# Graph attention by gathered rows, and a reordered first feed-forward stage, in a two-layer gated mixer on one Trainium2 core

## The chip, the core and the metric

The kernel runs on one core of one Trainium2 chip. The metric is the device time of one execution in microseconds (us). The core has five engines with an instruction stream each: TensorE (PE, matmuls into PSUM), VectorE (DVE), ScalarE (ACT, activations), GpSimd (POOL, which also issues indirect DMAs) and SyncE (SP, which issues the plain DMAs). The streams meet only in semaphores.

## The reference, cut to what matters

Inputs are x [4, 256, 256] and a context [4, 256, 64]; the tokens are 1024 rows, which the kernel holds as T = 8 tiles of 128. Four residual steps follow each other, each scaled with the tanh of a gate:

```python
x = x + tanh(g_xattn[0]) * graph_attention(ctx, layernorm(x))   # two layers, 8 heads of 32
x = x + tanh(g_ffn[0])   * ternary_ffn(layernorm(x))            # 256 -> 704 -> 256, silu(g) * u
x = x + tanh(g_xattn[1]) * learned_adjacency(ctx, layernorm(x))
x = x + tanh(g_ffn[1])   * moe(layernorm(x))                    # 8 experts, top 2, 256 -> 512 -> 256

# one graph layer; adj is layernorm(x), N x N
e = leaky_relu(attn_self[:, :, None] + attn_neigh[:, None, :]) + MASK_VAL * (1.0 - adj)
out = elu(softmax(e) @ feat + b)          # MASK_VAL = -1e10

# learned adjacency: sim is N x N per batch from two 64 x 64 products of the context
threshold = top_k(sim, 76)[..., -1:]
A = sigmoid(sim) * (sim >= threshold)
out = (1 - gamma) * adj + gamma * (A + A.T) / 2
```

With a mask of 1e10 times the entry, the softmax of the graph attention is 1 at the largest entry of the row of `adj` and 0 elsewhere as long as that entry leads by enough. So each graph layer gives node n the features of the one node idx(n), the position of the largest entry in row n. Both kernels use this, and check on the chip that it holds; if it does not, they branch to a general path, which this input never takes.

## The kernel before, in words

The first three steps run over all tokens in two halves of four tiles (HT = 4, HN = 512 tokens); a half is two of the four batches. The order of all of it is one list, SCHEDULE (L333), written out by hand: every engine walks the same list and issues its own part of each step that has one, so on every engine an instruction waits behind all that stands before it in the list. On VectorE, a second list, FILL (L767), puts steps of the top-k search behind named steps.

Graph part. `pick h` (VectorE) takes the LayerNorm of x, scales it to the mask, finds each row's maximum and writes `hot`, the one-hot matrix. `graph_hot` transposes it on TensorE. `graph_first` gathers the context rows by a matmul with it, `graph_hidden` is the first layer's product with its exp on ScalarE, `hidden_elu` its ELU, `graph_feat` (L1353, four tiles of 272 columns) the second layer's product, `graph_out` (L1363) gathers those rows, again by a matmul; `graph_elu` and `add_graph` end it. `logit_check` looks at the logits' size. `graph_check h` turns a flag into a branch on TensorE, ScalarE and VectorE, once per half: VectorE writes `flag` at L1045, then loads it and branches.

Learned adjacency, beside this. `queries` and `sims` compute `sim` for all tokens (ScalarE copies it out). The threshold is found by guess and correction: `spread` takes each row's mean and variance, `count n` (ScalarE, L584, one activation with a sum per tile) counts the entries above the guess, `move n` corrects it; then the search of `below` (five steps for each pair of tiles and a closing one, 21 in all) takes the top 16 below the guess. `lost` and `keep 0` check that the threshold is among them, with a branch around a full search that is written out for eight tiles (`search_in_full`, L850), and multiply the mask in. `sigmoids` (L589) is a tanh, a copy. `kept h` transposes the result.

Feed-forward part. `norm_ffn h` normalises, `turn_ffn h` transposes on TensorE and copies on ScalarE. `ffn_up h it` (TensorE L1448, ScalarE silu L655, VectorE gate L1066) is one of six up products of a half: four matmuls of 512 columns, two for the last. A product needs the gate of the product two before it, since it has two PSUM banks. The gate of the second half has one wait more:

```python
                if h == 1:
                    dve.wait_ge(down_done, 1)
```

since it overwrites `hT`, which the down product of the first half still reads. `ffn_down p` is the down product (L1467, 24 matmuls of 256 columns per half); VectorE multiplies it with `dsr` and adds it to x (L1084, L1088). Parts p are the first half, and two quarters of the second. `attn_stats`, `attn`, `moe_stats`, `norm_moe`, `turn_moe`, `router` and `choices` follow, the first half's beside the second half's up products.

POOL raises variances to the power -1/2 (L459) for each LayerNorm, and to 1/2 once for `spread` (L455), in a fixed order. SP loads all inputs, then experts 0 and 1; experts 2, 3, 4 and 7 wait for `graph_over` (both halves' graph part added), 5 and 6 for the last down product, as the FFN's weights lie in their place.

The expert part (L1150 onward in VectorE, L1520 onward in TensorE) sorts tokens into blocks, gathers each block's rows by indirect DMA and runs 19 blocks. The change does not touch it.

## Time and profile before

| what | us |
|---|---|
| median of 3 runs | 289.89 (289.8 to 295.19) |
| profiled execution | 290.8 |
| its span in the trace | 289.1 |
| TensorE busy | 231.3 |
| VectorE busy | 129.6 |
| ScalarE busy | 71.1 |
| POOL busy | 68.4 |
| first FFN up product starts | 62.60 |
| first down product | 87.92 to 98.55 |
| second down product | 124.57 to 135.21 |
| first gather of the expert part starts | 163.75 |

The span runs from the first to the last instruction of the profiled execution; its own time is 1.7 us longer than the span. "Busy" is the time in which an instruction of that engine runs; a busy matmul row is not TensorE at its peak, since a row's end is modelled.
### The profile page before, as it was taken

The numbers are of one execution on the slowest core, as the hardware profiler recorded it, in microseconds if no ns is written. First come the engines' busy times: TensorE is split into PE (matmuls) and PEld (weight loads), VectorE is DVE, ScalarE is ACT, GpSimd is POOL, SyncE is SP. The second block draws the span as 40 slices with busy tenths as digits, with TensorE's granted clock in tenths as the row PEclk, the third lists the DMA queues.
The fourth block names the chain that finished last, engine by engine and source line by source line (L and its number), as shares of the span: only waits on it lengthen the run. The fifth ranks groups of instructions, "written<-read, shape, count | busy, mean of one in ns | idle before, by whom it ended". The sixth has DMA issues, their size and how long they took to land.

```text
span 289.1 us, 3573 instructions
## 1 busy us (share of the span) xinstructions
PE 231.3 (80%) x1246; PEld 180.7 (63%) x1247; DVE 129.6 (45%) x407; ACT 71.1 (25%) x144; POOL 68.4 (24%) x84
## 2 busy tenths in 40 slices
PE   3979996469988997997071269999999999999950
PEld 3648575344347743575061169998999999986540
DVE  2779558779884478236948832000100100100100
ACT  1444654531120021200032011232123123123210
POOL 5010200100100011000210211355345435545442
PEclk9999999658999999999655559999999999999995
DMA  6797000009920002201950010223322422311200
GB/s 172 268 363 291 0 1 0 3 15 356 415 88 2 0 2 74 73 0 39 362 180 0 19 39 20 36 36 51 63 36 36 60 42 36 53 24 19 25 5 1
DMA packets 15829, 23.88 MB, mean 83 GB/s; under 512 B 4989, under 2 KB 11648, under 8 KB 15808
## 3 DMA queue, kind: packets, MB, share of 16 engines
q1 hardware_dynamic: 10400, 19.02, 18.2%
q0 software_dynamic: 3744, 4.20, 9.1%
q10 hardware_dynamic: 1664, 0.40, 0.6%
q8 instruction: 11, 0.18, 0.3%
q14 instruction: 10, 0.08, 0.1%
HBM read 20.07 MB, written 4.59 MB: 85 GB/s over the span
## 4 chain that ended last, share of the span: by engine, by line
PE 65%; DVE 19%; DMA 4%; issue 3%; POOL 3%; ACT 2%; DVEq 1%; POOLq 0%; ACTq 0%
PE PS L1551 19%; PE PS L1560 9%; PE PS L1467 7%; PE PS L1456 6%; PE PS L1566 4%; DMA zc<-xn_rows,idsu 3%; PE PS L1358 3%; DVE stat L753 2%; PE PS L1436 2%; PE PS L1291 2%; PE PS L1503 2%; PE PS L1544 2%; DVE xn L1055 2%; DVE hT L1074 2%; PE PS L1349 1%
## 5 line engine op out<-in xcount | busy, mean ns | idle before, releaser
L1551 PE MATMUL PS<-hT,e 128*128 128x128 f32 x512 | 64.0, 280 | 0.5 <-ACT hT L681 0.5
L1551 PEld LDWEIGHTS PS<-hT,e 128*128 128x128 f32 x512 | 62.3, 196 | 1.6 <-ACT hT L681 0.9
L1273 DVE TENSOR_TENSOR hT<-th,PS 128x512 f32<-128x512 f32 x19 | 13.1, 687 | 87.9 <-PE PS L1551 73.0
L1456 PE MATMUL PS<-xnT,e 128*128 128x512 f32 x88 | 41.3, 623 | 3.1 <-ACT xnT L644 1.8
L459 POOL TENSOR_TENSOR rstd<-veps,nhalf 128x4 f32<-128x4 f32 (+1 forms) x10 | 9.1, 911 | 119.1 <-DVE veps L758 119.1
L475 POOL DMA_INDIRECT out_dram<-hT,idsu x16 | 25.5, 1591 | 44.0 <-ACT hT L694 41.0
L1456 PEld LDWEIGHTS PS<-xnT,e 128*128 128x128 f32 x88 | 17.1, 200 | 23.5 <-issue 19.6
L1560 PE MATMUL PS<-e,hT 128*128 128x256 f32 x128 | 30.3, 379 | 0.0
L1560 PEld LDWEIGHTS PS<-e,hT 128*128 128x128 f32 x128 | 23.2, 190 | 2.9 <-issue 0.5
L466 POOL DMA_INDIRECT zc<-xn_rows,idsu x16 | 16.9, 1056 | 29.7 <-DVE idsu L1228 18.4
L1467 PE MATMUL PS<-e,hT 128*128 128x256 f32 x96 | 21.3, 381 | 2.1 <-DVE hT L1074 2.1
L694 ACT ACTIVATE hT<-PS,coef 128x256 f32<-128x256 f32 x19 | 9.0, 475 | 54.1 <-PE PS L1560 46.0
L1467 PEld LDWEIGHTS PS<-e,hT 128*128 128x128 f32 x96 | 18.1, 190 | 4.8 <-DVE hT L1074 2.5
L664 ACT ACTIVATE th<-PS,gs 128x512 f32<-128x512 f32 (+1 forms) x12 | 8.2, 686 | 44.3 <-PE PS L1456 44.3
L686 ACT ACTIVATE th<-PS 128x512 f32<-128x512 f32 x19 | 11.4, 598 | 29.0 <-PE PS L1551 25.4
L1436 PE MATMUL PS<-ident,xn 128*128 128x128 f32 x32 | 6.3, 354 | 15.0 <-DVE xn L1055 15.0
L1436 PEld LDWEIGHTS PS<-ident,xn 128*128 128x128 f32 x32 | 4.8, 181 | 17.4 <-DVE xn L1055 16.9
L1291 PE MATMUL PS<-ident,ones 128*128 128x128 f32 x44 | 8.4, 375 | 8.6 <-POOL b1x L449 4.6
L753 DVE BATCH_NORM_STATS2 stat<-x 128x6 f32<-128x256 f32 x32 | 11.4, 414 | 6.8 <-POOL b1x L449 4.6
L1544 PE MATMUL PS<-ident,zc 128*128 128x128 f32 x40 | 8.0, 283 | 6.4 <-DMA zc<-xn_rows,idsu 6.4
L1291 PEld LDWEIGHTS PS<-ident,ones 128*128 128x128 f32 x44 | 7.9, 282 | 8.3 <-POOL b1x L449 4.3
L1566 PE MATMUL PS<-e,hT 128*128 x24 | 11.3, 593 | 0.0
(232 smaller groups left out, 285.6 us busy)
## 6 DMA issues: line engine op xcount, KB each, us to landing
e<-e_in SPq DMA_DIRECT2D x24, 512.0 KB, 7.5
x<-x_in SPq DMA_DIRECT2D x2, 512.0 KB, 6.4
e<-gw_in SPq DMA_DIRECT2D x1, 768.0 KB, 9.4
e<-uw_in SPq DMA_DIRECT2D x1, 640.0 KB, 9.2
...
out_dram<-x SPq DMA_DIRECT2D x2, 256.0 KB, 5.3
```

What stands on the lines that cost most here:

```text
L466: pool.indirect_dma_start(out=xg[q], out_offset=None, in_=xn3_dram, in_offset=bass.IndirectOffsetOnAxis(ap=ids, axis=0), bounds_check=boun ...
L475: pool.indirect_dma_start(out=out, out_offset=bass.IndirectOffsetOnAxis(ap=ids, axis=0), in_=yv[q], in_offset=None, bounds_check=bound, oo ...
L753: ins = dve.bn_stats(stat[:, at + i, :], src[:, i, :])
L1273: dve.tensor_tensor(hh[me], th[:, me, :], PS[:, 2 + me, :], ALU.mult).then_inc(gated, 1)
L1291: pe.matmul(PS[:, 7, 0:P], ones[:, :], ident[:, :], start=True, stop=True)
L1436: mm = pe.transpose(PS[:, bank + k, i * P:(i + 1) * P], xn[:, at + i, k * P:(k + 1) * P], ident[:, :])
L1456: mm = pe.matmul(PS[:, bank, :], w[:, k, it * P:(it + 1) * P], xnT[:, h, k, :], start=(k == 0), stop=(k == 1))
L1467: mm = pe.matmul(PS[:, 4 + i // 2, (i % 2) * 256:(i % 2 + 1) * 256], hT[:, it, i * P:(i + 1) * P], dw[:, it, :], start=(it == 0), stop=(it ...
L1544: mm = pe.transpose(PS[:, 4, q * 256 + k * P:q * 256 + (k + 1) * P], xg[q][:, k * P:(k + 1) * P], ident[:, :])
L1551: mm = pe.matmul(PS[:, bank + q, f * P:(f + 1) * P], w[:, k * F + f * P:k * F + (f + 1) * P], xgT[q][:, k, :], start=(k == 0), stop=(k == 1))
L1560: mm = pe.matmul(PS[:, 6 + q, 0:C], hh[q][:, f * P:(f + 1) * P], W2[j // 2][:, f * C:(f + 1) * C], start=(f == 0), stop=(f == F // P - 1))
L1566: mm = pe.matmul(PS[:, bank + q, :], xgT[q][:, k, :], w[:, bass.ds(at + k * F, F)], start=(k == 0), stop=(k == 1))
```

## The change

1. The graph part is turned round. Both layers' products are computed for every context token without a gather in front (`hidden`, `feat`), the bias comes in as a one-row matmul, the ELU follows, and the finished rows of each batch are stored to DRAM (`graph_rows0` to `3`). `choice` takes idx from the one-hot matrix by a matmul with the node numbers, `compose` applies it twice, `index` makes it an integer, and `gather_rows` (POOL, one indirect DMA per tile) fetches the rows; `add_graph` adds them to x tile by tile, with the LayerNorm's `bn_stats` between. `pick` works on x itself, without LayerNorm and mask. The one-hot matrices are bf16.
2. The checks are one for all: sums of squares (`sum_x`, `sum_ctx`, `sum_hidden`, and in `weights`, on ScalarE) bound the logits, `lead` the margin, one matmul adds them up (`flag`), and there is one `graph_check`.
3. `queries` multiplies the two 64 x 64 weights first (`mix`), so that `sims` needs one product of the context, not two.
4. The second half's second graph layer (`feat 1,0` and `1,1`), its ELU, store and gather stand behind the first FFN up product. `spread`, `guess`, `count`, `move`, `sigmoids`, the search, `lost` and `keep` run per half and stand later in the list; the full search is written as loops.
5. `dsr` is multiplied into the down weights by POOL (`scale_down`), so `ffn_down` on VectorE is one addition.
6. TensorE's warm-up starts as soon as `ones` is there and does not wait for the other constants; the eight warm-up matmuls at `turn_ffn` go. The first ACT table is loaded by an exp ahead of the work.
7. SP loads the context and first weights first, holds the FFN's weights back until x has landed, stores the four graph batches, and only then loads experts 0 and 1.

The diff, cut to its core:

```diff
+        SCHEDULE = [("hidden", 0), ("sum_x", 0), ("hidden", 1), ("hidden_elu", 0), ("pick", 0), ("feat", 0, 0),
+                    ("feat_elu", 0, 0), ("hot", 0), ("feat", 0, 1), ("hidden_elu", 1), ("choice", 0), ("mix", 0),
+                    ("compose", 0), ("weights", 0), ("feat_elu", 0, 1), ("index", 0), ("gather_rows", 0), ("queries", 0),
+                    ("sum_ctx", 0), ("sum_x", 1), ("pick", 1), ("sum_hidden", 0),
+                    ("sims", 0), ("gates", 0), ("lead", 0), ("hot", 1), ("flag", 0), ("graph_check", 0),
+                    ("add_graph", 0), ("choice", 1), ("compose", 1), ("norm_var", 0),
+                    ("norm_ffn", 0), ("scale_down", 0), ("turn_ffn", 0), ("index", 1), ("scales", 0),
+                    ("ffn_up", 0, 0), ("feat", 1, 0), ("feat_elu", 1, 0), ("feat", 1, 1), ("feat_elu", 1, 1),
+                    ("gather_rows", 1), ("spread", 0), ("spread", 1), ("ffn_up", 0, 1), ("guess", 0), ("count", 0, 0),
+                    ("guess", 1), ("add_graph", 1), ("norm_var", 1), ("ffn_up", 0, 2), ("norm_ffn", 1), ("move", 1, 0),
+                    ("count", 1, 0), ("count", 0, 1), ("turn_ffn", 1), ("ffn_up", 0, 3), ("move", 2, 0), ("move", 1, 1),
+                    ("count", 1, 1), ("sigmoids", 0),
+                    ("ffn_up", 0, 4), ("ffn_up", 0, 5), ("move", 2, 1), ("sigmoids", 1),
+                    ("ffn_up", 1, 0), ("ffn_down", 0), ("attn_stats", 0), ("lost", 0), ("keep", 0), ("kept", 0),
+                    ("ffn_up", 1, 1), ("attn", 0), ("moe_stats", 0), ("ffn_up", 1, 2), ("norm_moe", 0),
+                    ("ffn_up", 1, 3), ("turn_moe", 0), ("router", 0),
+                    ("ffn_up", 1, 4), ("choices", 0), ("lost", 1), ("keep", 1), ("ffn_up", 1, 5),
+                    ("kept", 1), ("ffn_down", 1), ("attn_stats", 1),
                     ("ffn_down", 2), ("attn_stats", 2), ("attn", 1), ("attn", 2), ("moe_stats", 1),
                     ("moe_stats", 2), ("norm_moe", 1), ("turn_moe", 1), ("turn_moe", 2), ("norm_moe", 2),
                     ("router", 1), ("router", 2), ("choices", 1), ("choices", 2)]
 
         order = lambda names: {stage: n for n, stage in enumerate(s for s in SCHEDULE if s[0] in names)}
...
+            for b in range(B):
+                sp.wait_ge(token_ready, b + 1)
+                sp.dma_start(f_dram[b].rearrange("(t p) c -> p t c", p=P),
+                             feat[:, 2 * b:2 * b + 2, :]).then_inc(feat_stored[b], 16)
+            sp.wait_ge(graph_over, HT)
             for e in range(2):
                 load_expert(e)
 
-            sp.wait_ge(graph_over, 2)
+            sp.wait_ge(graph_over, T)
             for e in (2, 3, 4, 7):
                 load_expert(e)
...
+            def gather_rows(h):
+
+                pool.wait_ge(index_ready, h + 1)
+                for b in range(2 * h, 2 * h + 2):
+                    pool.wait_ge(feat_stored[b], 16)
+                    for t in range(2 * b, 2 * b + 2):
+                        pool.sem_inc(pool_passed)
+                        pool.indirect_dma_start(
+                            out=picked[:, t, :], out_offset=None, in_=f_dram[b],
+                            in_offset=bass.IndirectOffsetOnAxis(ap=gix[:, t:t + 1], axis=0),
+                            bounds_check=last_node, oob_is_err=False).then_inc(row_picked[t], 16)
+
+            def scale_down(h):
+
+                pool.wait_ge(gates_tanh, 1)
+                pool.wait_ge(ffn_loaded, 16 * 7)
+                own(pool.tensor_scalar(dsr[:, :], dsr[:, :], tg[:, 2:3], None, ALU.mult))
+                pool.tensor_tensor(dw[:, :, :], dw[:, :, :], dsr[:, :].unsqueeze(1).to_broadcast([P, IT, C]),
+                                   ALU.mult).then_inc(dw_scaled, 1)
...
+            def sum_hidden(h):
+
+                act.wait_ge(h0_ready, 4)
+                for n, col in ((0, 1), (1, 4)):
+                    ins = act.activation(xnT[:, n, :, :], h0T[:, :, n * HN:(n + 1) * HN], ACT.Square, accum_out=norms[:, col:col + 1])
+                ins.then_inc(norms_ready, 1)
...
+            def graph_feat(h, p):
+                act.wait_ge(feat_done, 2 * h + p + 1)
+                act.activation(z[h][:, p * HN:(p + 1) * HN], PS[:, FEAT_BANK[h] + p, :], ACT.Exp).then_inc(feat_exp, 1)
...
-            FILL = {("move", 2): 3, ("deviation", LN["norm_ffn", 0]): 1, ("graph_check", 1): 6,
-                    ("ffn_up", 0, 0): 4, ("ffn_up", 0, 1): 2, ("ffn_up", 0, 2): 2, ("ffn_up", 0, 3): 4,
-                    ("ffn_up", 0, 4): 5, ("ffn_up", 0, 5): 3, ("ffn_up", 1, 5): 1}
+            FILL = {("move", 2, 0): 2, ("ffn_up", 0, 4): 3, ("ffn_up", 0, 5): 3, ("move", 2, 1): 2,
+                    ("ffn_up", 1, 0): 3, ("ffn_up", 1, 1): 2, ("ffn_up", 1, 2): 2, ("ffn_up", 1, 3): 3,
+                    ("ffn_up", 1, 4): 3}
...
             def keep(h):
 
-                if h == 0:
-                    search(STEPS)
-                    dve.wait_ge(lost_counted, 1)
-                    dve.tensor_scalar(flag[:, 2:3], PS[:, 6, 0:1], 1.0, None, ALU.min).then_inc(lost_ready, 1)
-                    dve.wait_ge(lost_ready, 1)
-                    with dve.If(dve.value_load(flag[0:1, 2:3], min_val=0, max_val=1)):
-                        search_in_full()
-                    dve.wait_ge(sig_ready, 1)
+                search(STEPS, h)
+                dve.wait_ge(lost_counted, h + 1)
+                dve.tensor_scalar(flag[:, 1 + h:2 + h], PS[:, 6, 0:1], 1.0, None, ALU.min).then_inc(lost_ready, 1)
+                dve.wait_ge(lost_ready, h + 1)
+                with dve.If(dve.value_load(flag[0:1, 1 + h:2 + h], min_val=0, max_val=1)):
+                    search_in_full(h)
+                dve.wait_ge(sig_ready, h + 1)
                 for t in range(h * HT, (h + 1) * HT):
...
+            def feat_elu(h, p):
+
+                t = h * HT + 2 * p
+                zp = z[h][:, p * HN:(p + 1) * HN]
+                dve.wait_ge(feat_exp, 2 * h + p + 1)
+                own(dve.tensor_scalar(zp, zp, 1.0, 1.0, ALU.min, ALU.subtract))
+                dve.tensor_tensor(feat[:, t:t + 2, :].rearrange("p t c -> p (t c)"), PS[:, FEAT_BANK[h] + p, :], zp,
+                                  ALU.max).then_inc(token_ready, 1)
+
+            def index(h):
+
+                cols = slice(h * HT, (h + 1) * HT)
+                dve.wait_ge(composed, h + 1)
+                dve.tensor_scalar(gix[:, cols], PS[:, 0, 8:8 + HT], float(N - 1), None, ALU.min).then_inc(index_ready, 1)
 
             def add_graph(h):
...
+
+                if h == 0:
+                    dve.wait_ge(gates_tanh, 1)
+                for i in range(HT + 1):
+                    t = h * HT + i
+                    if i < HT:
+                        dve.wait_ge(row_picked[t], 16)
+                        dve.scalar_tensor_tensor(out=x[:, t, :], in0=picked[:, t, :], scalar=tg[:, 0:1], in1=x[:, t, :],
+                                                 op0=ALU.mult, op1=ALU.add).then_inc(graph_over, 1)
+                    if i:
+                        dve.wait_ge(graph_over, t)
+                        ins = dve.bn_stats(stat[:, i - 1, :], x[:, t - 1, :])
+                own(ins)
...
             def ffn_down(p):
                 t, n = PARTS[p]
                 bank = 4 + (t % HT) // 2
-                y = z[0][:, 0:n * C]
-                xp = xr[:, t:t + n, :].rearrange("p t c -> p (t c)")
+                xp = xr[:, t:t + n, :]
                 dve.wait_ge(down_done, p + 1)
-                dve.tensor_tensor(y.rearrange("p (t c) -> p t c", t=n),
-                                  PS[:, bank:bank + n // 2, :].rearrange("p b (t c) -> p (b t) c", t=2),
-                                  dsr[:, :].unsqueeze(1).to_broadcast([P, n, C]), ALU.mult).then_inc(down_read, 1)
+                dve.tensor_tensor(xp, xp, PS[:, bank:bank + n // 2, :].rearrange("p b (t c) -> p (b t) c", t=2),
+                                  ALU.add).then_inc(down_read, 1)
                 dve.wait_ge(down_read, p + 1)
-                own(dve.tensor_tensor(xp, xp, y, ALU.add))
...
+            def graph_feat(h, p):
+                pe.wait_ge(h0_ready, 2 * h + 2)
+                if h == 0 and p == 0:
+                    pe.wait_ge(w1_loaded, 16 * 2)
+                for i in range(2):
+                    t = h * HT + 2 * p + i
+                    to = PS[:, FEAT_BANK[h] + p, i * C:(i + 1) * C]
+                    pe.matmul(to, ones[0:1, :], b1[0:1, :], start=True, stop=False)
+                    for k in range(2):
+                        mm = pe.matmul(to, h0T[:, k, t * P:(t + 1) * P], w1x[:, k, 0:C], start=False, stop=(k == 1))
+                mm.then_inc(feat_done, 1)
...
             def turn_ffn(h):
-                if h == 0:
-
-                    open_clock_gate(WARM_UP_FFN)
-                turn_tokens(XT["turn_ffn", h], 6, 0, HT)
+                turn_tokens(XT["turn_ffn", h], FFN_TURN_BANK, 0, HT)
                 if h == 0:
                     pe.wait_ge(ffn_loaded, 16 * 7)
...
             def ffn_down(p):
                 t, n = PARTS[p]
                 pe.wait_ge(ffn_h_ready, IT * (t // HT + 1))
+                if p == 0:
+                    pe.wait_ge(token_ready, 4)
+                    pe.wait_ge(dw_scaled, 1)
...
             def lost(h):
 
                 pe.wait_ge(xnT_copied, XT["turn_ffn", 1] + 1)
-                pe.wait_ge(found_ready, 1)
-                pe.matmul(PS[:, 6, 0:1], ones[:, :], found[:, 1, 1:2], start=True, stop=True).then_inc(lost_counted, 1)
+                if h == 1:
+                    pe.wait_ge(scores_read, 1)
+                pe.wait_ge(found_ready, h + 1)
+                pe.matmul(PS[:, 6, 0:1], ones[:, :], found[:, 1, 2 * h + 1:2 * h + 2], start=True, stop=True)\
+                  .then_inc(lost_counted, 1)
```

## Rows read from the trace of the kernel before

**Rows 1.** Page, parts 1 and 2: TensorE's busy time, and its granted clock in 40 slices

```profile
PE 231.3 (80%) x1246; PEld 180.7 (63%) x1247; DVE 129.6 (45%) x407; ACT 71.1 (25%) x144; POOL 68.4 (24%) x84
...
PEclk9999999658999999999655559999999999999995
```

**Rows 2.** Chain of waits in order of time: start us, length us, engine, tile, line, count

```profile
58.60 1.97 PE PS L1436 x8
...
64.39 0.90 DVE work L805 x4
...
67.81 0.75 DVE top L824 x2
...
87.92 10.63 PE PS L1467 x48
...
107.58 1.39 DVE x L1110 x4
...
124.57 10.64 PE PS L1467 x48
...
135.24 0.70 DVE zb L1084
...
163.75 4.04 DMA zc<-xn_rows,idsu
```

**Rows 3.** Windows of PE: stretch, length, busy (count), granted clock, DMA share, GB/s

```profile
53.00:54.00 1.00, 1.00 (x9) 0.71 0.12 25
...
67.00:68.00 1.00, 1.00 (x4) 0.96 0.88 303
...
138.00:140.00 2.00, 0.00 (x0) 0.69 0.99 395
```

**Rows 4.** Timeline, first 30 us: start, busy, engine, line, operation, count, idle before

```profile
3.25 0.52 POOL L444 MEMSET zc<- 128x512 f32 x1
...
4.64 5.48 PE L1291 MATMUL PS<-ident,ones 128*128 128x128 f32 x28 [4.64 <-POOL b1x L449]
...
20.23 1.27 ACT L609 ACTIVATE zb<-PS,b 128x512 f32<-128x512 f32 x2 [2.14 <-PE PS L1349]
...
24.35 1.41 DVE L922 SCALAR_TENSOR_TENSOR h0T<-PS,b,zb 128x512 f32<-128x512 f32 x2
...
29.13 1.64 POOL L455 TENSOR_TENSOR row_dev<-row_mv,half_power 128x8 f32<-128x8 f32 x1 [10.85 <-DVE row_mv L781]
```

**Rows 5.** Timeline from 50 to 63 us, same columns

```profile
50.99 0.15 DVE L1045 TENSOR_SCALAR flag<-PS 128x1 int32<-128x1 f32 x1
...
52.70 1.28 DVE L959 SCALAR_TENSOR_TENSOR x<-zb,tg,x 128x1024 f32<-128x1024 f32 x1 [1.56 <-issue]
...
54.02 1.41 DVE L753 BATCH_NORM_STATS2 stat<-x 128x6 f32<-128x256 f32 x4
...
57.17 1.38 DVE L1055 TENSOR_SCALAR xn<-x,mv,rstd 128x256 f32<-128x256 f32 x4 [0.34 <-POOL rstd L459]
...
60.61 1.02 ACT L644 ACTIVATE xnT<-PS 128x1024 f32<-128x1024 f32 x1 [4.64 <-PE PS L1436]
...
61.80 1.28 ACT L659 ACT_TABLE_LOAD   x1 [0.16 <-issue]
...
62.60 7.63 PE L1456 MATMUL PS<-xnT,e 128*128 128x512 f32 x12 [1.80 <-ACT xnT L644]
```

**Rows 6.** Timeline from 68 to 182 us, same columns

```profile
91.49 3.26 DVE L878 SCALAR_TENSOR_TENSOR a<-sim,bar,a 128x256 f32<-128x256 f32 x8 [3.44 <-issue]
...
99.25 13.90 PE L1456 MATMUL PS<-xnT,e 128*128 128x512 f32 x32
```

**Rows 7.** Page, part 5: one group: count, busy us, mean ns, idle before

```profile
L466 POOL DMA_INDIRECT zc<-xn_rows,idsu x16 | 16.9, 1056 | 29.7 <-DVE idsu L1228 18.4
```

**Rows 8.** Groups by line and form, the same columns: the counting activation

```profile
L584 ACT ACTIVATE a<-sim,bar 128x256 f32<-128x256 f32 x16 | 7.9, 495 | 0.5 <-DVE bar L786 0.5
```

**Rows 9.** DMA issues by line: count, size of one, median us from issue to landing

```profile
xn_rows<-xn SPq DMA_DIRECT2D x2, 256.0 KB, 3.1
```

680 lines of the change are left out of this document (362 added, 318 removed).

## The prediction

> **What bounds the kernel now.** I read the page first: TensorE is busy 231 of 289 us, nearly solid from 168 us on, and its clock line has two dips, at 50 to 65 and 137 to 170 us [rows 1]. Then the chain of waits, for the borders of stages: `turn_ffn` at 58.60, the first down product at 87.92, the second at 124.57, its end at 135.24, the first gather of the expert stage at 163.75 [rows 2]. Behind 135.24 the code changes only in one addition, so the change is decided in 0 to 135 us. That stretch has two parts. Up to the first FFN up product at 62.60 [rows 5] short steps alternate between TensorE, VectorE and ScalarE, and latency bounds it. From 62.60 to 135.24 the products follow each other and VectorE's work, the top-k search above all, lies beside them. The profiled execution took 290.8 us, its span is 289.1, the median of the runs 289.89: I work in the trace's times and put the difference on the median.
>
> **Prices.** An up product (8 records) 13.90/4 = 3.47 us, the half-size sixth 1.73; a 256-column product 10.63/24 = 0.44 [rows 2, 6]. A gate 0.74; four `bn_stats` 1.41, then aggregate, power and wait until the normalising starts 1.74 (57.17 - 55.43), four normalisings 1.38; a copy or square of 1024 elements 1.02; a flag to the next VectorE operation 1.56 [rows 5]. Five search steps run from 64.39 to 68.56: 0.84 each [rows 2]. ScalarE's exp of 512 elements 0.64, VectorE's PSUM operation on 512 0.71, a `tensor_scalar` on 512 0.4 by halving one on 1024 [rows 4]. Four counting activations 2.0 [rows 8]. A 256 KB store lands after 3.1 [rows 9], a gather takes POOL 1.06 [rows 7] and lands 4.0 after it starts [rows 2].
>
> **The head: FFN start 62.6 -> 41.6.** The two gathers by matmul, the second-layer product per half, `logit_check`, the second flag and the warm-up of `turn_ffn` go. The new order: 28 warm-up records start with `ones` at 1.1 instead of 4.64 and take 5.5 [rows 4]: 6.6. Two 512-column products, exp (ScalarE is free of its table load at 7.9), two ELU halves of 0.4 + 0.7: `h0T` ready at 10.9. `max` and `hot` 2.6 more, `feat 0,0` (six 256-column products, with the bias row) to 13.7, ELU to 15.6; `feat 0,1` to 17.2; `choice`, `compose` 19.2; `index` 19.5; four gathers behind the store of 19.2, landed by 28. They are hidden: ScalarE is later. It copies weights and queries to 23.1, then squares 1024-element tiles four times (1.2 each with the accumulator's read) to 28.0; `flag`'s matmul needs the last of them and one `sim` copy: 28.9. Seven small VectorE operations 30.45, branch 31.95 [rows 5]. `add_graph` with `bn_stats` 4 x (0.45 + 0.36): 35.3; 1.74 to `norm_ffn`: 37.0 to 38.4; transposes at the low clock 1.97 [rows 2], copy 1.02: first up product at 41.6. A late bias load or POOL's new constants would make it 44, shorter squares 39.
>
> **The clock.** In the trace it drops in the second after 53.0, 5 us behind the last dense products, again in 138 to 140, some 3.5 us behind those of 135.2, and comes back in 67 to 68 after the stream that began at 62.60 [rows 3, 5]. Each return costs 4.4 us of stream at half speed, 2.2 us. I charge that at the start, once for every stall over 8 us, and half for stalls near 5.
>
> **First half of the FFN.** All engines follow one written order, so I look for the place where each waits. `ffn_up 0,0` ends at 47.2 (low clock), `feat 1,0` and `1,1` (12 x 0.44) at 52.5, `ffn_up 0,1` and `0,2` at 59.4. Then TensorE stands in `turn_ffn 1`: exp and ELU 54.45, store 57.6, two gathers more on POOL 59.9, where the two powers of `spread` are queued behind them, 61.9; `guess 1` 62.3; `add_graph 1` 65.7; normalised 68.7. **Stall 1: 9.3 us.** The tables of Exp and Silu change twice more, at 1.28 each [rows 5], inside ScalarE's idle time; cover gone they would cost 2.6. Sign and Tanh ran under Exp's first table; should Tanh need it again between the silus, `sigmoids 0` would add up to 2.6 to stall 2. I take none. `turn_ffn 1` and `ffn_up 0,3` end at 75.3; TensorE has 5.2 us of products left. `ffn_up 0,4` gives its hidden tile only after gate 0.7, `move 2,0` 0.8, two steps 1.7, `move 1,1` 0.8, `count 1,1` 2.0, `sigmoids 0` 2.1, silu 0.7, gate 0.7: 84.9. **Stall 2: 4.5 us.** `ffn_up 1,0` to 89.9 with half a clock charge, the down product 10.6: 100.5. The kernel before has its first down product, `kept` and `ffn_up 1,0` done at 98.55 + 0.9 + 3.5 = 102.9.
>
> **Second half.** The gate of `ffn_up 1,0` waits for the down product (`down_done`), and all that is queued behind it on VectorE too. From 100.5: gate 0.7, last step of the search 1.55 and two more 1.7, the sum of the down product 1.25, `attn_stats` 2.0, then `keep 0`: flag 0.2, branch, 1.63 for four masks. The branch took 3.44 before [rows 6]; its body is now three short loops, so between 1.2 and 3.4 I take 1.4, the flag's. TensorE stands in `kept 0` until 111.0. **Stall 3: 10.5 us**; before, this work lay under the down product. With `kept 0` and the low clock `ffn_up 1,1` ends at 117.6. VectorE then needs gate, two steps, `attn 0` 3.25 (1.39 of it the scaling [rows 2]), `moe_stats` 2.0, gate, two steps, `norm_moe` 1.35, so 11.4; TensorE has two products, 6.9: **stall 4: 4.5.** `turn_moe` and `router` now stand side by side with a copy of 1.0 between; with clock charges `ffn_up 1,4` ends at 138.2. Then gate, last steps 2.4, `choices` 1.2, `keep 1` 3.2, against 1.7 of products: **stall 5: 5.7**; `kept 1` ends at 146.9, and the down products, half a charge more, at 159.0. The tail saves one addition: 0.7, as long as the one at 135.24 [rows 2].
>
> Sum: 159.0 - 135.2 - 0.7 = +23.1: head -21.0, stalls +34.5, moved products +5.3, and +4.3 that is some 9 of clock charges less the waits that this stretch has already. On the median 289.9 that is **313 us**.
>
> POOL's `scale_down`, 1536 elements with two inputs, has no row. Below: a fill at 0.52 per 512 [rows 4] gives 1.6; above: the power, 1.64 for 8 elements [rows 4], gives 315. I take three times the fill, 4.7, as the nearest row by kind; over 18 us it would hold up `gather_rows 1`.
>
> The Trainium skill (GPSIMD Engine Reference, Specifications and Performance versus the Vector engine) says that VectorE and GpSimd share their SBUF interfaces and that a two-input operation costs about 2.6 cycles an element, an estimate of 3.3 us here. No row has both engines in long operations at once. By that rule `norm_ffn 0`, which starts beside `scale_down`, would finish late: rival A.
>
> **Rivals.**
> A. *POOL holds VectorE.* `norm_ffn 0` waits up to the 4.7 us: 317.5. For: same moment, 37 us. Against: nothing in the trace either way. Chance 0.10.
> B. *The second half stays covered.* If stalls 3 to 5 cost no more than the waits in the kernel before, only the first half counts: 101.4 against 102.9, so -1.5 - 0.7: 288. It decides on whether VectorE reaches `keep 0` before the down product ends. Against: the `down_done` wait in the gate. 0.10.
> C. *Early start kept.* TensorE bounds the FFN as before: 41.6 + 62.0 + 5.3 = 108.9 against 124.6: -15.7 - 0.7: 273.5. This is the other side: from the point where VectorE's added work (moves 3.2, spreads and guesses 4.4, the graph's sum 3.2, its ELU 2.2, four search steps and a second closing step 5: 18 us) fits beside the products. For: VectorE is busy only 45% [rows 1]. Against: each stall follows from the order on one engine. 0.10.
> Forecast 0.70.
>
> **Range.** The forecast's own: head +-3, each stall +-1.5, clock charges -5 to +3: 300 to 322. Down to 288 it takes in B; C and the tails stay out. Faster by over 2% 0.10 (C), within 2% 0.10 (B), slower 0.80; 2% is about what a measurement of this kernel can tell from no change.
>
> **What would show it.** First up product near 41.6; TensorE idle 9 us ahead of `turn_ffn 1` with VectorE's wait on POOL or the gathered rows; idle 10 us between the first down product and `kept 0`; the clock line with dips at 60 to 72 and 100 to 115 us. Wrong if the first down product starts before 85, or `kept 0` follows it within 3 us, or the expert stage changes its length of 125 us.

## The result, and the profile after

The changed kernel takes 335.0 us (median of 4, 331.08 to 336.46) against 291.87 for the kernel before on the same chip (289.8 to 295.19): a ratio of 1.146, 95% interval 1.127 to 1.165. The forecast was 313 with a range of 288 to 322: the direction was right, the size some 22 us short. Executions of one kernel differ in their mean granted clock (0.787 to 0.810 here) and with it in their time, which is why some medians below come with a wide spread. The profiled execution took 334.66 us, its span is 332.7, and that is 43.6 longer than the trace before, where 23.1 was forecast.

The page of the changed kernel, busy times, and in 40 slices of 8.3 us the granted clock and the DMAs' rate; the first two answer to [rows 1]:

```profile
PE 248.3 (75%) x1212; PEld 186.1 (56%) x1213; DVE 121.7 (37%) x393; ACT 76.8 (23%) x163; POOL 80.5 (24%) x96
...
PEclk9755555898596985895779555599999999999996
...
GB/s 181 223 166 81 16 2 0 3 116 388 366 388 3 0 0 3 0 66 60 0 0 57 357 95 0 47 18 32 50 46 54 43 51 37 56 29 32 16 9 0
```

TensorE has 34 fewer records and is busy 17 us longer: the work shrank, and so did the clock. Before, the clock line has its first dip at 50 us; here the dip begins at 12 us and lasts to 60.

TensorE's timeline up to the end of the second down product (start, busy, engine, line, operation, count, idle before), the groups that began after a wait of 1 us or more, with others between them left out, and the last line; they answer to [rows 2, 5]:

```profile
12.10 0.69 PE L1477 MATMUL PS<-b,ones 1*128 1x256 f32 x2 [1.71 <-DVE h0T L1049]
...
54.05 1.97 PE L1581 MATMUL PS<-ident,xn 128*128 128x128 f32 x8 [9.04 <-DVE xn L1193]
57.23 5.32 PE L1599 MATMUL PS<-xnT,e 128*128 128x512 f32 x8 [1.21 <-ACT xnT L738]
86.32 1.97 PE L1581 MATMUL PS<-ident,xn 128*128 128x128 f32 x8 [10.16 <-DVE xn L1193]
102.95 6.36 PE L1599 MATMUL PS<-xnT,e 128*128 128x512 f32 x8 [4.53 <-DVE hT L1214]
122.19 0.56 PE L1624 MATMUL PS<-found,ones 128*128 128x1 f32 x2 [2.52 <-DVE found L944]
130.14 1.94 PE L1637 MATMUL PS<-ident,a 128*128 128x128 f32 x8 [7.39 <-DVE a L996]
148.72 1.46 PE L1581 MATMUL PS<-ident,xn 128*128 128x128 f32 x8 [4.50 <-DVE xn L1193]
151.29 3.58 PE L1652 MATMUL PS<-rg,xnT 128*128 128x8 f32 x16 [1.11 <-ACT xnT L746]
164.12 0.56 PE L1624 MATMUL PS<-found,ones 128*128 128x1 f32 x2 [3.33 <-DVE sc L1275]
...
169.86 10.63 PE L1613 MATMUL PS<-e,hT 128*128 128x256 f32 x48
```

The first up product starts at 57.23, where the forecast had 41.6: that is 15.6 of the 22 us. Behind it stand the five stalls: 10.16 ahead of `turn_ffn 1`, 4.53 ahead of `ffn_up 1,0`, 2.52 + 0.56 + 7.39 from the first down product to `kept 0`, 4.50 ahead of `turn_moe 0`, and 3.33 ahead of `lost 1`, which the sixth up product at half clock (3.76), `keep 1` and `kept 1` follow. From the first up product to the end of the second down product it is 123.3 us, forecast 117.4. The expert stage is as before: its first gather starts 27.6 us behind the last down product (180.53 to 208.17), against 28.5 (135.24 to 163.75 in [rows 2]). So of the 20.5 us between the forecast and the trace, 15.6 lie in the head and 5.9 in this stretch, and behind it 1.0 was gained that was not forecast.

Now the head. TensorE's windows (stretch, length, busy and count, granted clock, DMA share, GB/s):

```profile
10.00:12.00 2.00, 0.39 (x1) 1.00 0.33 72
12.00:14.00 2.00, 1.90 (x5) 0.69 0.37 71
14.00:16.00 2.00, 2.00 (x5) 0.50 0.99 396
60.00:64.00 4.00, 4.00 (x12) 0.93 0.00 0
```

At 12 us the first products of the second graph layer begin with the bias, a matmul one row deep. In that window the clock goes from 1.00 to 0.50 (2.4 to 1.2 GHz), and it is back only in the last line, after 48 us. What that costs is seen in `sims` (L1446), timeline again:

```profile
32.86 7.19 PE L1446 MATMUL PS<-ctxT,th 64*128 64x256 f32 x16 [0.68 <-ACT th L631]
...
40.81 0.54 PE L1566 MATMUL PS<-norms,ones 128*128 128x6 f32 x2
```

The same sixteen records of `sims` took 3.61 before. The flag's matmul, forecast for 28.9, comes at 40.81.

And the end of the head, timeline of all engines, 48 to 54 us:

```profile
48.03 1.05 POOL L491 TENSOR_TENSOR rstd<-veps,nhalf 128x4 f32<-128x4 f32 x1 [14.87 <-DVE veps L857]
...
49.12 4.88 DVE L1193 TENSOR_SCALAR xn<-x,mv,rstd 128x256 f32<-128x256 f32 x4 [1.17 <-POOL rstd L491]
50.11 3.42 POOL L518 TENSOR_TENSOR e<-e,dsr 128x1536 f32<-128x1536 f32 x1
```

Four normalising operations, 1.38 in [rows 5], take 4.88: the longest of them takes 3.58 where the others take 0.40 to 0.41, and it ends behind POOL's product, which ends at 53.5.

### The profile page after: what moved, and what is told of

It reads as the page before. It is cut to its first block, busy times and chain, and to the rows that moved or that the text cites. A ratio compares the mean times of both kernels' runs of the same rounds, so it can differ in the third digit from the quotient of the medians.

```text
span 332.7 us, 3519 instructions
## 1 busy us (share of the span) xinstructions
PE 248.3 (75%) x1212; PEld 186.1 (56%) x1213; DVE 121.7 (37%) x393; ACT 76.8 (23%) x163; POOL 80.5 (24%) x96
## 4 chain that ended last, share of the span: by engine, by line
PE 59%; DVE 18%; issue 9%; DMA 4%; ACT 3%; POOL 3%; ACTq 2%; DVEq 0%; POOLq 0%
PE PS L1700 18%; PE PS L1599 9%; PE PS L1709 8%; PE PS L1613 6%; PE PS L1479 4%; PE PS L1715 3%; DVE xn L1193 3%; PE PS L1581 2%; PE PS L1652 2%; PE PS L1477 2%; DMA e<-graph_rows,gix 2%; DVE stat L848 2%; PE PS L1693 1%; POOL e L508 1%; DVE hT L1214 1%
## 5 line engine op out<-in xcount | busy, mean ns | idle before, releaser
L1599 PE MATMUL PS<-xnT,e 128*128 128x512 f32 x88 | 51.2, 744 | 5.7 <-DVE hT L1214 4.5
L1599 PEld LDWEIGHTS PS<-xnT,e 128*128 128x128 f32 x88 | 20.9, 246 | 31.5 <-issue 26.1
L491 POOL TENSOR_TENSOR rstd<-veps,nhalf 128x4 f32<-128x4 f32 (+1 forms) x8 | 7.1, 889 | 120.2 <-DVE veps L857 120.2
L1581 PE MATMUL PS<-ident,xn 128*128 128x128 f32 x32 | 7.6, 407 | 32.9 <-DVE xn L1193 32.9
L1581 PEld LDWEIGHTS PS<-ident,xn 128*128 128x128 f32 x32 | 5.6, 207 | 35.4 <-DVE xn L1193 35.4
L1214 DVE SCALAR_TENSOR_TENSOR hT<-th,us,PS 128x512 f32<-128x512 f32 (+1 forms) x12 | 8.9, 745 | 42.7 <-PE PS L1599 18.6
L789 ACT ACTIVATE hT<-PS,coef 128x256 f32<-128x256 f32 x19 | 9.0, 474 | 53.5 <-PE PS L1709 45.4
L508 POOL DMA_INDIRECT e<-graph_rows,gix x8 | 8.4, 1053 | 42.4 <-DVE gix L1066 22.8
L1479 PE MATMUL PS<-w1x,h0T 128*128 128x256 f32 x32 | 12.8, 539 | 0.0
L673 ACT ACTIVATE a<-sim,bar 128x256 f32<-128x256 f32 x16 | 7.9, 495 | 17.3 <-DVE bar L900 11.4
```

The lines of the kernel that those rows point to most:

```text
L508: pool.indirect_dma_start(out=picked[:, t, :], out_offset=None, in_=f_dram[b], in_offset=bass.IndirectOffsetOnAxis(ap=gix[:, t:t + 1], axi ...
L1214: dve.scalar_tensor_tensor(out=hT[at:P, it, :], in0=th[at:P, n % 2, :], scalar=us[at:P, it:it + 1], in1=PS[at:P, bank, :], op0=ALU.mult, o ...
L1479: mm = pe.matmul(to, h0T[:, k, t * P:(t + 1) * P], w1x[:, k, 0:C], start=False, stop=(k == 1))
L1581: mm = pe.transpose(PS[:, bank + k, i * P:(i + 1) * P], xn[:, at + i, k * P:(k + 1) * P], ident[:, :])
L1599: mm = pe.matmul(PS[:, bank, :], w[:, k, it * P:(it + 1) * P], xnT[:, h, k, :], start=(k == 0), stop=(k == 1))
```

## The experiments

In the diffs "-" is the changed kernel unless another is named. A step ("fill", n, bank) is n of the warm-up's matmuls (ones by ones, 128 columns) into a PSUM bank that is free there, in TensorE's order; they change no result. The bank number 13 stands for bank 3 behind one more wait.

### The bias with all rows (e1)

```diff
-                    pe.matmul(to, ones[0:1, :], b1[0:1, :], start=True, stop=False)
+                    pe.matmul(to, ident[:, :], b1[:, :], start=True, stop=False)
```

> The bias of the second graph layer comes in by a product with the identity, 128 rows deep, in place of one row of ones; the number and the width of the matmuls stay. Theory N (the granted clock falls at 12 to 14 us because the one-row matmuls leave TensorE nearly empty right behind an idle stretch): the clock stays at 1.00 through 12 to 30 us, the sims take 3.6 us in place of 7.19, the flag's matmul comes near 31 in place of 40.81, and the kernel gains 8 to 10 us: 325 to 327. Theory I (the idle time of 1.7 us and the light work around it let the clock fall, whatever the bias's depth): nothing changes, 333 to 336, the flag's matmul at 40 to 41.

Measured: 325.0 us (321.84 to 326.37), ratio to before 1.110 (1.096 to 1.124): 10 us gained by one operand. Its windows, all engines (busy of PE, PEld, DVE, ACT, POOL, then the clock):

```profile
12.00:14.00 2.00, 2.00 (x11) 1.77 (x10) 1.84 (x7) 0.00 (x0) 0.00 (x0) 1.00 0.42 98
...
18.00:20.00 2.00, 1.85 (x21) 1.73 (x22) 1.97 (x6) 0.32 (x5) 0.00 (x0) 1.00 1.04 290
20.00:22.00 2.00, 2.00 (x3) 0.46 (x2) 1.96 (x8) 1.00 (x7) 0.00 (x0) 0.53 0.81 264
```

And from its TensorE timeline:

```profile
45.02 1.97 PE L1581 MATMUL PS<-ident,xn 128*128 128x128 f32 x8 [9.06 <-DVE xn L1193]
```

The clock holds through the second layer's products and falls only at 20 us, after `choice`, `compose` and `weights`, whose matmuls have 1 and 16 columns. `turn_ffn 0` comes at 45.02 in place of 54.05. The flag's matmul comes at 31.77. The size is theory N's; that the sims take 3.6 us was wrong, since the clock had fallen by then (they take 7.19). The idle time ahead of the bias was also shorter here, 0.82 against 1.71 us. The runs on the warm-up, below, hold the two apart as far as the traces do.

### Matmuls in the waits of the head (e2)

```diff
-("hidden", 1), ("hidden_elu", 0)
+("hidden", 1), ("fill", 4, 3), ("hidden_elu", 0)
...
+("fill", 6, 4) behind ("flag", 0), ("fill", 16, 4) behind ("compose", 1)
```

> Warm-up matmuls of 128 columns stand in every wait that TensorE has in the head: 4 ahead of the first second-layer product, 2 to 4 at eight places up to the flag, 6 behind it, 16 ahead of the first transposes of the feed-forward part. Theory I (light work lets the clock fall): the granted clock stays at 1.00 through the head, the sims take 3.6 us, and the first up product starts near 48 in place of 57.23 at full speed: 10 to 13 us gained, 322 to 325. Theory W (whatever stands in the waits, the clock is lost because the warm-up at 1 us came too early and stopped before the dense part): the clock still falls at 12 to 14 us, the fillers lie in the way, and the time is 335 to 340.

Measured: 325.27 us (323.98 to 327.43), ratio 1.111 (1.099 to 1.123). The bias is one row deep here, and beside it the clock fell all the same, at 15 us; it came back between 18 and 19 us and stayed past 44:

```profile
16.00:18.00 2.00, 2.00 (x13) 1.85 (x13) 0.93 (x2) 0.60 (x1) 0.00 (x0) 0.50 1.06 381
18.00:20.00 2.00, 2.00 (x11) 1.27 (x9) 1.93 (x5) 1.09 (x2) 0.00 (x0) 0.85 1.12 319
...
36.00:40.00 4.00, 3.23 (x40) 3.15 (x41) 3.25 (x12) 0.17 (x1) 0.00 (x0) 1.00 0.03 8
```

The flag's matmul comes at 33.44 and the first up product starts at 49.60. So each of two different cures gives some 8 to 9 us in the head, the full-depth bias or matmuls in the waits; both together, below, give more.

### Down weights scaled earlier (e3)

```diff
-("gates", 0), ("lead", 0), ... ("norm_ffn", 0), ("scale_down", 0),
+("gates", 0), ("scale_down", 0), ("lead", 0), ... ("norm_ffn", 0),
```

> POOL's scaling of the down weights moves ahead of the flag, right behind the gates' tanh. Theory P (POOL's long two-input operation holds VectorE's normalising by their shared access to SBUF): the four normalising operations of the first half take 1.4 us in place of 4.88 and the first up product starts near 53.7: 3 to 3.5 us gained, 331 to 332; VectorE's small operations beside the scaling, at 38 to 43 us, get longer at most by a few tenths. Rival (the 4.88 us come from something else, the store or the weights' loads): they stay at 4.9, and the time at 335.

Measured: 332.92 us (328.76 to 336.24), ratio 1.128 (1.113 to 1.144), so 2 us by the medians, not to be told from none. The timeline tells more:

```profile
40.66 3.43 POOL L518 TENSOR_TENSOR e<-e,dsr 128x1536 f32<-128x1536 f32 x1
40.84 0.15 DVE L1028 TENSOR_SCALAR sums<-sums 128x1 f32<-128x1 f32 x1
41.03 3.07 DVE L1029 SCALAR_TENSOR_TENSOR sums<-sums 128x1 f32<-128x1 f32 x1
...
50.71 1.38 DVE L1193 TENSOR_SCALAR xn<-x,mv,rstd 128x256 f32<-128x256 f32 x4 [1.17 <-POOL rstd L491]
```

Normalising is back at 1.38, and a VectorE operation on one element per partition, 0.16 elsewhere, takes 3.07: it ends as POOL's product does. It stands on the flag's path, so the 3 us only moved. My expectation of "a few tenths" was wrong: this is not slower sharing, the operation is held until POOL's two-input operation is over. The Trainium skill (GPSIMD Engine Reference, Key points) names contention for VectorE instructions in a mode that uses two ports or with two SBUF inputs. The operation held here has two SBUF inputs, which agrees, and the trace adds how long: until the end. Whether the held normalising operation, which has one, uses two ports, no run here shows. Not every VectorE operation is held: `TENSOR_SCALAR` L1028, on one element, started at 40.84, 0.18 us behind POOL's product, and took 0.15.

### The gate that waits for the down product (e4)

```diff
-("ffn_up", 1, 0), ("ffn_down", 0), ("attn_stats", 0), ("lost", 0), ("keep", 0), ("kept", 0),
+("ffn_up", 1, 0), ("lost", 0), ("keep", 0), ("gate", 1, 0), ("ffn_down", 0), ("attn_stats", 0), ("kept", 0),
```

`gate` is VectorE's part of `ffn_up 1,0`, taken out of its place.

> VectorE's gate of the first up product of the second half, which waits for the down product, is taken out of its place and put behind lost 0 and keep 0; kept 0 moves behind the down product on TensorE. Theory S (stall 3 is the wait of everything queued behind that gate): VectorE ends the search and keep 0 below the down product, TensorE runs kept 0 right behind it, the stall of 10.5 us between the down product and kept 0 falls under 1 us, and with a half clock charge less the kernel gains 9 to 12 us: 323 to 326. Rival (VectorE's total of work bounds that stretch, so the waits only move): the idle time comes back ahead of turn_moe 0 or kept 1 and the gain is under 4 us: 331 or more.

Measured: 327.28 us (323.1 to 329.68), ratio 1.109 (1.093 to 1.124): 7.7 us gained by the medians.

```profile
112.97 0.55 PE L1628 MATMUL PS<-found,ones 128*128 128x1 f32 x2 [3.19 <-DVE found L944]
113.39 13.49 PE L1617 MATMUL PS<-e,hT 128*128 128x256 f32 x48
126.72 1.04 PE L1641 MATMUL PS<-ident,a 128*128 128x128 f32 x8
...
143.27 1.97 PE L1585 MATMUL PS<-ident,xn 128*128 128x128 f32 x8 [5.22 <-DVE xn L1193]
```

`kept 0` follows the down product without a gap, and stall 3 is gone. Two things I had left out: TensorE now waits 3.19 us ahead of the down product, for the search that `lost 0` needs, and with that idle time the down product runs partly at half clock (13.49 in place of 10.52). The gain is short of the 9 to 12 expected by this. The rival is out all the same: stall 4 grew by 0.7 only.

### Four edits together (e5)

The identity bias, the gate's place, fillers (2, 2, 3, 3, 6, 6, 12), and the scaling ahead of `sum_ctx`, meant for VectorE's wait for the squares.

> Four single edits together: the bias by a product with the identity, fillers in TensorE's waits of the head (fewer than before ahead of the flag), the gate that waits for the down product behind keep 0, and POOL's scaling of the down weights at 30 to 36 us, beside VectorE's wait for the squares. Theory A (the losses stand in different places and add): 8 to 10 us from the clock in the head, 3 from the normalising, 7 to 8 from stall 3: 335.0 - 20 = 313 to 317, with the first up product near 41 to 44 at full clock and the four normalising operations at 1.4 us. Theory B (TensorE's stretch behind the start hides part, since stalls 1 and 2 are set by VectorE): 320 to 324.

Measured: 311.69 us (310.62 to 311.9), ratio 1.072 (1.066 to 1.078): 23.3 us gained, a little more than theory A's sum. First VectorE and POOL beside the flag, then TensorE:

```profile
28.90 3.43 POOL L522 TENSOR_TENSOR e<-e,dsr 128x1536 f32<-128x1536 f32 x1
29.00 3.35 DVE L1029 TENSOR_TENSOR sums<-sums 128x1 f32<-128x1 f32 x1
...
43.43 3.67 PE L1614 MATMUL PS<-xnT,e 128*128 128x512 f32 x8 [1.20 <-ACT xnT L742]
```

The flag's matmul comes at 28.48, where the forecast had 28.9 and the changed kernel 40.81: with the clock kept up to there, the head's sum comes out. The normalising takes its 1.4 us again, but the contention is not gone: the flag's operations now stand beside the scaling, and the second of them, 0.16 elsewhere, takes 3.35. The first up product starts at 43.43, 1.8 us behind the forecast's 41.6, and 3.2 of that path is this hold. Stall 1 is untouched at 9.85.

### The second half's graph layer back in the head (e8)

```diff
+("sims", 0), ("feat", 1, 0), ("feat", 1, 1), ("feat_elu", 1, 0), ("feat_elu", 1, 1),
...
+("index", 1), ("gather_rows", 1), ("scales", 0), ("ffn_up", 0, 0),
-("feat", 1, 0), ("feat_elu", 1, 0), ("feat", 1, 1), ("feat_elu", 1, 1), ("gather_rows", 1),
```

> The bias by a product with the identity, and beside that only the reordering of the change undone in its first half: the second half's second graph layer stands in the head behind the sims, and its gathers right behind its index, ahead of the first up product. To be held against the run with the identity alone (325.0). Theory S (stall 1 is the chain store, gather, power, add_graph behind the first up product): the 9.9 us that TensorE waits ahead of turn_ffn 1 fall to 2 to 4, the head gets 4 to 6 us longer by the products and two exps, which took 6.8 us behind the first up product before: 317 to 319. Rival (the products in the head stand on the path one for one, at half clock 10 us, and VectorE's spreads and guesses alone keep norm_ffn 1 late): 323 to 327.

Measured: 322.65 us (320.9 to 324.76), ratio 1.109 (1.099 to 1.120); the run with the identity bias alone had 325.0. By itself this half of the change's title costs 2 us or nothing.

```profile
55.09 1.97 PE L1580 MATMUL PS<-ident,xn 128*128 128x128 f32 x8 [8.93 <-DVE xn L1192]
...
76.58 1.97 PE L1580 MATMUL PS<-ident,xn 128*128 128x128 f32 x8 [5.07 <-DVE xn L1192]
```

`turn_ffn 0` is 10.1 us later (55.09 against 45.02): the products stand on the path for 7.9 us, the first half of them at half clock, as the rival said, and TensorE then waits 2.56 more for VectorE's `norms`, which the order puts behind the two ELUs. From `turn_ffn 0` to `turn_ffn 1` it is 21.5 us in place of 31.8: 4.9 of it stall, 5.4 products. So of stall 1 about half is the chain store, gather, add. The other half is VectorE's own work behind the gate of `ffn_up 0,0`, spreads, guesses, the sum and its statistics, from 64.78 on nearly without a gap. Gain and loss cancel while the clock is low.

### Then at full clock, with the first half's order mended (e6)

Against e5: the graph layer in the head, and

```diff
+("spread", 0), ("ffn_up", 0, 0), ("spread", 1), ("guess", 0), ("count", 0, 0), ("ffn_up", 0, 1),
...
+("count", 1, 1), ("turn_ffn", 1), ("ffn_up", 0, 4), ("ffn_up", 0, 5), ("sigmoids", 0), ("move", 2, 1), ("sigmoids", 1),
```

> e5's edits, and the second half's graph layer in the head; spreads, guesses and counts are spread over the first up products, turn_ffn 1 stands behind ffn_up 0,3, sigmoids 0 behind ffn_up 0,5. Theory S: stalls 1 and 2 are both an effect of the order alone, TensorE waits under 3 us in the whole stretch from the first up product to the first down product, and that stretch takes 28 us in place of the 51.9 of the changed kernel less 6.8 of products gone: against e5 12 to 15 us gained, 299 to 304. Rival (VectorE's total, some 24 us of graph, guess and search work beside six products of 3.5, is too much for it): stalls of 5 us or more stay, 306 or more.

Measured: 304.62 us (303.01 to 306.36), ratio 1.048 (1.039 to 1.057), 7.1 gained. The stretch from the first up to the first down product took 41.95 us (49.07 to 91.02), where I had 28: stall 1 went to 2.40, but 1.57 and 5.66 stand ahead of `ffn_up 0,5` and `ffn_up 1,0`, and 3.07 ahead of `lost 0`. ScalarE's counts, two of 2.0 us in a row, now held up a silu. The gain is half of the 12 to 15 expected, and a stall over 5 us stayed, so it is mostly the rival's case: I had moved the wait and not the work.

### The second half's order mended too (e7)

`lost 1`, `keep 1` and `kept 1` ahead of `turn_moe 0`, eight search steps under the first down product, `choices 0` under the second, on top of the run before. `lost 1` and `kept 1` wait for `kept 0` to be read in place of the router's scores.

> e6, and the second half's order: eight steps of the search lie under the first down product, lost 1, keep 1 and kept 1 come before turn_moe 0, turn_moe 0 and router 0 before and behind the last up product, choices 0 under the second down product. Theory S (stalls 4 and 5 are VectorE's work in the wrong place, not too much of it): both go, some 9 us and the slow router's 2: 289 to 295, level with the kernel before. Rival (VectorE is bound there: 3.25 for attn, 2.0 of statistics, the two kept and keep, against five products of 3.5): TensorE still waits 5 us or more between the first and the second down product, 297 or more.

Measured: 297.4 us (294.18 to 300.52), ratio 1.015 (1.007 to 1.023). Stalls 4 and 5 went, but one of 7.32 us came in their place, since `lost 1` now stood earlier than the search could be done. The time lies where the two theories meet, and the stall is of the rival's size:

```profile
119.62 0.56 PE L1639 MATMUL PS<-found,ones 128*128 128x1 f32 x2 [7.32 <-DVE found L947]
```

### One order from end to end (e9)

It keeps the edits of the four together, with the identity bias, fillers (6, 2, 3, 3, 8), the scaling behind `gates` and the gate behind the down product, has other places for the search steps, and this order:

```diff
+("turn_ffn", 0), ("feat_elu", 1, 1), ("gather_rows", 1), ("scales", 0), ("spread", 0), ("ffn_up", 0, 0),
+("spread", 1), ("guess", 0), ("count", 0, 0), ("add_graph", 1), ("norm_var", 1), ("ffn_up", 0, 1), ("guess", 1),
+("count", 0, 1), ("norm_ffn", 1), ("ffn_up", 0, 2), ("move", 1, 0), ("count", 1, 0), ("ffn_up", 0, 3),
+("turn_ffn", 1), ("move", 1, 1), ("count", 1, 1), ("move", 2, 0), ("ffn_up", 0, 4), ("ffn_up", 0, 5),
+("move", 2, 1), ("ffn_up", 1, 0), ("sigmoids", 0), ("sigmoids", 1), ("ffn_down", 0), ("gate", 1, 0),
+("lost", 0), ("keep", 0), ("down_sum", 0), ("attn_stats", 0), ("ffn_up", 1, 1), ("ffn_up", 1, 2), ("kept", 0),
...
+("choices", 0), ("ffn_down", 1), ("down_sum", 1), ("lost", 1), ("keep", 1), ("attn_stats", 1),
+("ffn_down", 2), ("down_sum", 2), ("kept", 1),
...
-            sp.wait_ge(graph_over, HT)
+            sp.wait_ge(graph_over, T)
             for e in range(2):
```

> One order from end to end, with the changed kernel's cheaper parts. Head: the flag's matmul stands before the second half's last products and its check before their ELU; 6 fillers ahead of the first second-layer product. First half: counts behind the silus that they held up, add_graph 1 ahead of the gate of ffn_up 0,1, experts 0 and 1 loaded only when all rows are added. Second half: lost 0 behind the first down product on TensorE, kept 0 behind ffn_up 1,2, the second half's search beside the second down product with kept 1 as its last step. Theory S (the written order alone costs the time; VectorE's total fits beside the products): first up product near 46, first down product near 76, second down product ends near 120 to 124, expert stage 125 to 127 longer than that as before: 276 to 284, below the kernel before. Rival (VectorE or ScalarE bounds the stretch whatever the order): TensorE waits 10 us or more between the first up product and the end of the second down product, and the time is 288 or more.

Measured: 280.95 us (279.95 to 282.07), ratio 0.968 (0.963 to 0.973): faster than the kernel before. First up product 44.76, first down product 75.40, the second down product's end 124.4. TensorE's waits of 1 us and more between them are 2.16, 3.13 and 1.11 us. VectorE's work did fit: the five stalls were the order's. One loss stays in the head: the scaling again holds an operation of the flag's chain, for 3.10 us.

### Where the clock is lost: the warm-up alone (e10 and e11)

The kernel before, its warm-up on `ones` as soon as they are there:

```diff
-            pe.wait_ge(consts, CONSTS)
+            pe.wait_ge(ones_ready, 1)
             open_clock_gate(WARM_UP)
+            pe.wait_ge(consts, CONSTS)
```

> The kernel before, with only its warm-up as in the changed kernel: it starts at 1 us with the matrix of ones and ends at 6.5, 3.5 us ahead of the first products at 10. Theory W (an early warm-up that stops before the dense part loses the clock): the granted clock falls between 10 and 15 us, and the head takes 5 us or more longer: 295 or more. Theory I (what counts is the light work behind, which the kernel before does not have there): the clock stays at 1.00 up to 50 us and the time stays at 290 to 292.

Measured: 301.18 us (292.72 to 301.57); three of four executions took 301, with a mean granted clock of 0.854 to 0.864, and one 292.7, with 0.884, so no ratio is given. The profile is of the one that took 301.57:

```profile
10.00:12.00 2.00, 0.00 (x0) 0.00 (x0) 1.93 (x7) 1.78 (x6) 0.00 (x0) 0.68 0.79 263
12.00:14.00 2.00, 1.85 (x8) 1.57 (x8) 1.10 (x7) 1.04 (x2) 0.00 (x0) 0.50 1.04 396
```

From its TensorE timeline:

```profile
12.15 1.97 PE L1332 MATMUL PS<-ident,e 128*128 128x128 f32 x8 [2.48 <-DVE e L898]
```

There is no one-row matmul in this kernel, and the clock falls in an idle stretch of 2.48 us: with the early start TensorE is through with `queries` before VectorE has `hot`. In the kernel before the warm-up lay in that wait, and `queries` began at 10.05, when nothing was late behind them.

The changed kernel, its warm-up behind the constants again:

```diff
-            pe.wait_ge(ones_ready, 1)
-            open_clock_gate(WARM_UP, 7)
             pe.wait_ge(consts, CONSTS)
+            open_clock_gate(WARM_UP, 7)
```

> The changed kernel with only its warm-up as in the kernel before, behind all constants (about 4.5 us, so it ends near 10). Theory W (an early warm-up followed by an idle stretch loses the clock): it stays at 1.00 past 20 us, the hidden products start some 3 us later, and in the sum 4 to 7 us are gained: 328 to 331. Theory L (the light work in the head loses it whenever the warm-up is): it falls near 16 us as in the changed kernel, and the time is 335 to 339.

Measured: 337.44 us (326.23 to 338.1), again three near 338 (clock 0.793 to 0.798) and one at 326 (0.836), no ratio. In the profile, of 338.1 us, the idle time ahead of the bias is 0.63 us, and the clock falls all the same, at 16 us, beside the one-row matmuls:

```profile
14.00:16.00 2.00, 1.37 (x5) 0.78 (x5) 1.97 (x6) 1.41 (x4) 0.00 (x0) 1.00 1.02 409
16.00:18.00 2.00, 2.00 (x6) 0.79 (x4) 1.24 (x5) 0.00 (x0) 0.00 (x0) 0.56 1.08 361
```

With an idle stretch about as short, 0.82, the identity bias kept it to 20. But the identity bias does not keep it by itself. In the run with the second half's order mended the idle stretch is 1.70 us, as long as in the changed kernel, and the clock falls in it (TensorE's timeline, then its windows):

```profile
12.01 1.22 PE L1492 MATMUL PS<-b,ident 128*128 128x256 f32 x2 [1.70 <-DVE h0T L1052]
...
11.00:12.00 1.00, 0.00 (x0) 0.63 0.12 26
...
18.00:19.00 1.00, 1.00 (x8) 0.95 1.06 358
```

It is back at 18 us, with nothing but the layer's own products in between; beside the one-row bias the changed kernel had to wait until 60. In e6, with 0.94 idle, it fell too, and was back at 15. So the clock fell in idle stretches (2.48 and 1.70 us) with no one-row matmul near; and with one-row matmuls behind the idle stretch it fell after as little as 0.63 us, and did not come back beside them, except in e2, where fillers stood between. One-row matmuls are not enough for a fall either: those of the second half, at 62 to 69 us in the changed kernel, run right behind an up product at full clock (64 to 68 us: 1.00). How much of the 10 us of e1 is due to its shorter idle stretch alone, no run shows. One execution in four of each of the last two kernels was 8 to 12 us shorter than the others; these have no trace, only their higher mean clock.

### The same order, with the gaps filled (e12)

Here "-" is the run before (e9).

```diff
-("hot", 1), ("graph_check", 0), ... ("fill", 8, 3), ("norm_var", 0), ... ("turn_ffn", 0), ("feat_elu", 1, 1),
+("hot", 1), ("fill", 8, 13), ("graph_check", 0), ... ("fill", 14, 3), ("norm_var", 0), ... ("turn_ffn", 0), ("fill", 4, 3), ("feat_elu", 1, 1),
```

> The kernel of the last order with three more groups of fillers, ahead of the graph check (8), ahead of (14 in place of 8) and behind (4) turn_ffn 0. In the run before it the granted clock was 0.57 in 36 to 40 us and 0.50 in 44 to 48. Theory: the clock stays at 1.00 to 70 us, the first up products take 13.9 for four from the start, and 2 to 4 us are gained: 277 to 279. Rival: the fillers lie in the way of the first transposes and the gain is eaten: 280 to 282.

Measured: 275.54 us (274.61 to 279.26), ratio 0.937 (0.928 to 0.946), the best of all. The clock on its page, in slices of 6.8 us:

```profile
PEclk9999999999999995995555599999999999999995
```

A piece of VectorE's timeline beside POOL's scaling, and TensorE's to the end of the second down product:

```profile
30.89 0.16 DVE L1025 COPY sums<-PS 128x6 f32<-128x6 f32 x1 [3.51 <-PE PS L1581]
31.09 2.88 DVE L1026 TENSOR_TENSOR sums<-sums 128x1 f32<-128x1 f32 x1
...
114.39 5.43 PE L1628 MATMUL PS<-e,hT 128*128 128x256 f32 x24
```

Up to 123 us one slice is below 9, at 103 to 109 us, where the router stands. The second down product ends at 119.8 in place of 135.2. The first up product starts at 45.08 against 62.60, and from there to the end of the second down product it is 74.7 us against 72.6: the whole gain over the kernel before is the head. That the gathered rows and the single check are what shortens it is argued; no run takes them apart from the other changes there. POOL's scaling (30.52 to 33.95) still holds an operation of the flag's chain for 2.88 us; a place for it where VectorE has nothing to do was not tried in this order. As the changed kernel was ordered, it lost the whole gain and 43 us more.

## Why the prediction was right and wrong

- **Head, 62.6 -> 41.6: wrong, 57.23.** The failed step is the clock's charge: "I charge that at the start, once for every stall over 8 us, and half for stalls near 5", with nothing inside the head, since in the kernel before the clock fell only "5 us behind the last dense products". Here it was at half from 13 to 60 us, and the flag's matmul came at 40.81 in place of 28.9: 11.9 us. With identity bias and fillers it came at 28.48, so the sum of operations up to there was right within 0.5. Each of the two cures alone had it at 31.77 and 33.44.
- **`scale_down`: size near, effect wrong.** The product took 3.42 against the 4.7 taken, with `dsr` 4.35 (the prediction's other estimate, 3.3, was nearer). "POOL holds VectorE", rival A, got 0.10 and was true: 3.5 us longer normalising on the path, within the "up to the 4.7" of its price. It should have stood in the main line, since the prediction had both operations at the same moment. This is the second failed step of the head, and with it 11.9 + 3.5 = 15.4 of the 15.6 us are accounted for.
- **Stall 1, 9.3: 10.16.** Right in place and cause, VectorE on POOL and the gathered rows. The term that was small is the gather's landing: 4.0 in [rows 2], 6.5 here (last one issued 75.37, used 81.92), with experts 0 and 1 loading at the same time (388 GB/s in the page's slices). The median of these four gathers is 6.4 us from issue to landing, and 2.9 for the four of the first half, which have no expert loads beside them; in e9, where the loads wait, it is 2.8. Of the stall the chain of rows is about half.
- **Stall 2, 4.5: 4.53. Stall 4, 4.5: 4.50. Stall 3, 10.5: 10.5** (119.67 to 130.14), with the `down_done` wait as its cause, which the gate's move shows. The branch took 1.23 (1.4 taken).
- **Stall 5, 5.7:** `kept 1` started 7.3 us behind `ffn_up 1,4` (160.8 to 168.1), forecast 7.4 with the 1.7 of the sixth up product. VectorE's chain was as worked out. TensorE's part was not, by luck without effect: the sixth up product took 3.76 at half clock and filled 2 us of the stall.
- **Clock charges in the stretch, some 9: too small by 4 to 5.** The router took 3.58; first product to first down product 51.9 in place of 48.3, and 71.3 in place of 69.1 behind it. The failed term is "half for stalls near 5": behind the 4.53 us stall `ffn_up 1,0` took 6.36 in place of 3.47, so 2.9 where 1.1 was charged, as much as behind a long one. Two ends of the sum stand 0.4 later than their terms give (84.9 + 3.47 + 1.1 is 89.5, not 89.9; 146.9 + 10.6 + 1.1 is 158.6, not 159.0); that was on the right side, and luck.
- **Exp and Silu tables:** hidden, as said; Tanh and Sign needed none.
- **Rival C** (TensorE bounds it, 273.5) is what the mended order came to, 275.5, with fillers that the rival did not have: VectorE's 18 us do fit. It was the written order that did not let them.

In short, of the 20.5 us that the trace was longer than forecast, 12 are the head's clock, 3.5 POOL's hold on VectorE, and 6 clock and landing in the stretch behind, less 1 behind all of it. What the experiments show of the cause is the cost of the low clock; what made it fall at 12 us is shown only as far as the runs on the bias and the warm-up go.
